# Head of the last stage of a decoder layer: second tile's scores directly behind the first's, its h turned on TensorE

## The reference, cut to what matters

```python
x = x + fake_quant(layernorm(x)) @ fake_quant(ctx)        # cross product, K = 1024
h = layernorm(x)
scores = (h @ Wq_w.T) @ keys.T                            # router: 16 wide, then 64 experts
gate = softmax over the 16 best scores, 0 elsewhere
z = h @ A_w.T                                             # 512 = 64 experts x 8
x = x + (z * gate) @ B_w.T * 2
```

## Time and profile before

| what | value |
|---|---|
| runs of before, us | 1106.42, 1109.94, 1109.15 (median 1109.15) |
| profiled execution, us | 1110.08, its span 1108.3 |
| TensorE busy | 1064.9 us, 96% of the span |
| VectorE busy | 905.2 us, 82% |
| ScalarE busy | 530.3 us, 48% |
| mean granted TensorE clock | 0.989 |

### The profile page before, as it was taken

One profiled execution on the slowest core, in us unless ns is written; L12 is line 12 of the kernel. 1 busy time (PEld: TensorE's weight loads), 2 busy tenths in 40 slices (PEclk: granted clock), 3 DMA queues, 4 the chain that ended last, 5 costly groups with the idle time before them and its releaser, 6 DMA issues.

```text
span 1108.3 us, 19648 instructions
## 1 busy us (share of the span) xinstructions
PE 1064.9 (96%) x6229; PEld 568.7 (51%) x6236; DVE 905.2 (82%) x1861; ACT 530.3 (48%) x1081; POOL 411.6 (37%) x423
## 2 busy tenths in 40 slices
PE   4999998999999999999999999999999998969998
PEld 3876544555555555555555555555555554434443
DVE  6789578988787978787888888787978798888973
ACT  4646366555454445454544455454545453233420
POOL 2049755534353434343442434353434243000000
PEclk8999999999999999999999999999999999989999
DMA  8016145654544445454545554554445378224442
GB/s 315 1 58 257 77 88 136 164 117 110 139 123 114 106 123 136 110 132 116 139 100 124 132 117 112 132 123 114 106 126 136 83 187 230 101 43 82 102 99 86
DMA packets 229601, 135.74 MB, mean 122 GB/s; under 512 B 200112, under 2 KB 202288, under 8 KB 228656
## 3 DMA queue, kind: packets, MB, share of 16 engines
q1 hardware_dynamic: 229552, 135.11, 48.1%
HBM read 68.23 MB, written 17.83 MB: 78 GB/s over the span
## 4 chain that ended last, share of the span: by engine, by line
PE 85%; DVE 8%; ACT 3%; issue 2%; DMA 1%; POOL 1%; SPq 0%; DVEq 0%; ACTq 0%; POOLq 0%
PE ps L1672 81%; PE ps L1924 2%; ACT prob L1034 1%; DVE wo_sb L1188 1%; DVE h_b L1188 1%; DVE prob L1397 1%; PE ps L1995 1%; DMA wq_sb<-wo_in 1%; DVE prob_t L1188 1%; DMA o_t<-in_wdown 1%; PE ps L1686 0%; ACT prob L890 0%; DVE stats L1196 0%; ACT wo_sb L807 0%; DVE wq_sb L1188 0%
## 5 line engine op out<-in xcount | busy, mean ns | idle before, releaser
L771 POOL TENSOR_SCALAR prob<-prob,row_inv 128x128 f32<-128x128 f32 (+3 forms) x256 | 203.5, 815 | 438.0 <-DVE row_inv L1368 438.0
L1672 PE MATMUL ps<-wo_sb,o_t 128*128 128x512 f16 x1536 | 353.0, 380 | 3.6 <-DVE x_sb L1379 3.6
L1672 PE MATMUL ps<-h_b,wq_sb 128*128 128x512 f16 x1524 | 344.9, 381 | 0.0
L1034 ACT ACTIVATE prob<-prob,neg_max 128x128 f32<-128x128 f32 (+3 forms) x256 | 140.6, 550 | 220.8 <-DVE neg_max L1403 220.8
L1672 PEld LDWEIGHTS ps<-h_b,wq_sb 128*128 128x128 f16 x1524 | 148.4, 98 | 178.2 <-issue 4.4
L1672 PEld LDWEIGHTS ps<-wo_sb,o_t 128*128 128x128 f16 x1536 | 147.6, 98 | 173.1 <-DVE x_sb L1379 6.3
L1379 DVE SCALAR_TENSOR_TENSOR x_sb<-ps,x_sb 128x512 f32<-128x512 f32 x256 | 174.2, 686 | 54.8 <-PE ps L1672 53.9
L1672 PE MATMUL ps<-prob_t,v_sb 128*128 128x128 f16 (+2 forms) x960 | 116.6, 274 | 6.5 <-DMA prob_t<-prob_s 6.5
L1672 PE MATMUL ps<-k_t,q_t 128*128 128x512 f16 (+3 forms) x768 | 114.8, 299 | 0.6 <-DVE neg_max L1403 0.5
L1397 DVE CUSTOM_DVE_ANT_0 prob<-ps,mask 128x512 f32<-128x512 f32 (+3 forms) x256 | 110.3, 484 | 2.3 <-issue 1.6
L1672 PEld LDWEIGHTS ps<-prob_t,v_sb 128*128 128x128 f16 x960 | 83.5, 98 | 36.8 <-DMA prob_t<-prob_s 7.3
(11 more groups left out here) (146 smaller groups left out, 1138.4 us busy)
## 6 DMA issues: line engine op xcount, KB each, us to landing
wq_in<-in_wq SPq DMA_DIRECT2D x64, 256.0 KB, 3.5
wo_in<-in_wo SPq DMA_DIRECT2D x32, 512.0 KB, 3.9
side_in<-in_ctx SPq DMA_DIRECT2D x16, 512.0 KB, 4.3
kv_parts<-wo_sb SPq DMA_DIRECT2D x7, 1024.0 KB, 5.0
x_sb<-in_x SPq DMA_DIRECT2D x8, 512.0 KB, 9.2
ctx_quantised<-side_out SPq DMA_DIRECT2D x16, 256.0 KB, 2.9
h_b<-ctx_quantised SPq DMA_DIRECT2D x2, 2048.0 KB, 10.8
out<-x_sb SPq DMA_DIRECT2D x8, 512.0 KB, 2.9
```

What stands on the lines that cost most here:

```text
L771: ins = nc.gpsimd.tensor_scalar(at, at, row_inv[:, u % 2, q:q + 1], S_P, ALU.mult, ALU.mult)
L1034: ins = nc.scalar.activation(at, at, ACT.Exp, bias=neg_max[:, n % 2, q:q + 1], scale=SOFTMAX, accum_out=row_sum[:, n % 2, q:q + 1])
L1672: ins = nc.tensor.matmul(out_, lhs(i), rhs(j), start=start and n == 0, stop=stop and n == 3 * len(pairs) - 1)
```

## The change

Only the last stage changes. On TensorE the h of tile 1 is now also turned there (`turn_h3(1)`, placed inside the z matmuls of `scores(0)`), `scores(1)` follows `scores(0)` directly, `x_product(2)` comes after it, and `scores(2)` moves behind `out_product(1)`. In every `scores` the keys now stand behind 6 matmuls of z, not 12. Thirteen matmuls whose result nobody reads (`fill`) stand around `turn_h3(0)`. The lists of ScalarE, VectorE and SyncE are written out by hand for tiles 0 to 3 to go with it; from i = 4 on the loop is as before. `gate_z` is the old body of the loop made a function. The diff, with that body left out on both sides:

```diff
--- before.py
+++ after.py
@@ -93,7 +93,12 @@
 
 def h3_dmas(t):
 
-    return 32 * ((t + t % 2) // 2)
+    return 32 * (t // 2)
+
+
+def h3_splits(t):
+
+    return 2 * t + 2 if t < 2 else t + 3
 
 
 def x_dmas(t):
@@ -108,6 +113,7 @@
 
 R_COL, S_COL = 0, P
 STEPS_AHEAD = 2
+TURN_FILL, ROUTER_FILL = 6, 7
 
 
 UNITS = GROUP * BATCH
@@ -629,12 +635,10 @@
                 sp.dma_start_transpose(blocks(x_qt[:, t % 2, :]), x_q[:, t % 2, :]).then_inc(x_landed[t % 2], 16)
 
             def turn_h3(t):
-                sp.wait_ge(h3_hi, t + 2)
-                sp.wait_ge(x_done, 2)
-                if t >= 2:
-                    sp.wait_ge(z_done, t - 1)
+                sp.wait_ge(h3_hi, h3_splits(t))
+                sp.wait_ge(z_done, t - 1)
                 sp.dma_start_transpose(blocks(h3_t[:, t % 2, 0, :]), h3_s[:, t % 2, 0, :]).then_inc(h3_landed[t % 2], 16)
-                sp.wait_ge(h3_lo, t + 2)
+                sp.wait_ge(h3_lo, h3_splits(t))
                 sp.dma_start_transpose(blocks(h3_t[:, t % 2, 1, :]), h3_s[:, t % 2, 1, :]).then_inc(h3_landed[t % 2], 16)
 
             def turn_gated(t):
@@ -645,18 +649,29 @@
                 sp.wait_ge(zt_lo, t + 1)
                 sp.dma_start_transpose(blocks(z_t[:, t % 2, 1, :]), z_s[:, t % 2, 1, :]).then_inc(z_landed[t % 2], 16)
 
+            def store(t):
+                sp.wait_ge(out_done, 2 * t + 2)
+                sp.dma_start(out[t], x_sb[:, t, :]).then_inc(stored, 16)
+
             turn_rounded(2)
-            for i in range(1, TT + STEPS_AHEAD):
+            turn_gated(0)
+            turn_rounded(3)
+            turn_gated(1)
+            turn_h3(2)
+            turn_rounded(4)
+            store(0)
+            turn_h3(3)
+            store(1)
+            turn_gated(2)
+            turn_rounded(5)
+            for i in range(4, TT + STEPS_AHEAD):
                 if i < TT:
                     turn_h3(i)
                 if i - 1 < TT - 1:
                     turn_gated(i - 1)
                 if i + STEPS_AHEAD < TT:
                     turn_rounded(i + STEPS_AHEAD)
-                if i >= 2:
-                    t = i - 2
-                    sp.wait_ge(out_done, 2 * t + 2)
-                    sp.dma_start(out[t], x_sb[:, t, :]).then_inc(stored, 16)
+                store(i - 2)
             sp.wait_ge(stored, 16 * TT)
 
         @block.gpsimd
@@ -1121,23 +1136,23 @@
 
             def h3_apply(t):
                 act.wait_ge(rstd3_done, t + 1)
-                if t == 2:
-                    act.wait_ge(h3_turned, 2)
-                if t >= 3:
-
-                    act.wait_ge(h3_hi, t)
-                    act.wait_ge(h3_lo, t)
+                if t in (2, 3):
+                    act.wait_ge(h3_turned, 2 * (t - 1))
+                if t >= 4:
+
+                    act.wait_ge(h3_hi, h3_splits(t - 2))
+                    act.wait_ge(h3_lo, h3_splits(t - 2))
                 nc.scalar.activation(h3[t % 2], x_sb[:, t, :], ACT.Identity, bias=h3_bias[:, t:t + 1],
                                      scale=rstd1[:, 2, 2 * TT + t:2 * TT + t + 1]).then_inc(h3_done, 1)
 
             def h3_high(t):
-                if t == 0:
+                if t < 2:
                     for j in range(2):
-                        act.wait_ge(h3_turned, j + 1)
-                        split_hi(h3_t[:, 0, 0, j * HALF:(j + 1) * HALF], ps[:, H_BANK[j], :], h3_hi, S_H)
+                        act.wait_ge(h3_turned, 2 * t + j + 1)
+                        split_hi(h3_t[:, t, 0, j * HALF:(j + 1) * HALF], ps[:, H_BANK[j], :], h3_hi, S_H)
                     return
                 act.wait_ge(h3_done, t + 1)
-                if t >= 3:
+                if t >= 4:
 
                     act.wait_ge(h3_landed[t % 2], h3_dmas(t - 2))
                 split_hi(h3_s[:, t % 2, 0, :], h3[t % 2], h3_hi, S_H)
@@ -1152,26 +1167,46 @@
                     act.wait_ge(z_landed[t % 2], z_dmas(t - 2))
                 split_hi(z_s[:, t % 2, 0, :], gated, zt_hi, 1.0)
 
-            h3_apply(0)
-            h3_high(0)
-            scale_rows(STEPS_AHEAD)
-            for i in range(1, TT + 1):
-                if i > 1:
-                    copy_small(i - 1)
-                if i < TT:
-                    h3_apply(i)
-                if i == 1:
-                    copy_small(0)
-                    sum_rows(STEPS_AHEAD)
-                t = i - 1
+            def weigh(t):
                 act.wait_ge(best_done, t + 1)
                 nc.scalar.activation(weight[:, t % 2, :], score[:, t % 2, :], ACT.Exp, bias=neg_best[:, t % 2:t % 2 + 1])\
                     .then_inc(weighted, 1)
+
+            h3_apply(0)
+            h3_high(0)
+            copy_small(0)
+            h3_apply(1)
+            h3_high(1)
+            scale_rows(2)
+            weigh(0)
+            sum_rows(2)
+            z_high(0)
+            scale_rows(3)
+            copy_small(1)
+            weigh(1)
+            z_high(1)
+            sum_rows(3)
+            h3_apply(2)
+            h3_high(2)
+            scale_rows(4)
+            sum_rows(4)
+            h3_apply(3)
+            h3_high(3)
+            scale_rows(5)
+            copy_small(2)
+            weigh(2)
+            z_high(2)
+            sum_rows(5)
+            for i in range(4, TT + 1):
+                copy_small(i - 1)
+                if i < TT:
+                    h3_apply(i)
+                weigh(i - 1)
                 if i < TT:
                     h3_high(i)
                 if i + STEPS_AHEAD < TT:
                     scale_rows(i + STEPS_AHEAD)
-                z_high(t)
+                z_high(i - 1)
                 if i + STEPS_AHEAD < TT:
                     sum_rows(i + STEPS_AHEAD)
 
@@ -1585,13 +1620,13 @@
                                                ALU.mult, ALU.mult).then_inc(rstd3_done, 1)
 
             def h3_split(t):
-                if t == 0:
+                if t < 2:
                     for j in range(2):
                         at = slice(j * HALF, (j + 1) * HALF)
-                        dve.wait_ge(h3_hi, j + 1)
-                        split_lo(h3_t[:, 0, 1, at], ps[:, H_BANK[j], :], h3_t[:, 0, 0, at], h3_lo, S_H)
+                        dve.wait_ge(h3_hi, 2 * t + j + 1)
+                        split_lo(h3_t[:, t, 1, at], ps[:, H_BANK[j], :], h3_t[:, t, 0, at], h3_lo, S_H)
                     return
-                dve.wait_ge(h3_hi, t + 2)
+                dve.wait_ge(h3_hi, h3_splits(t))
                 split_lo(h3_s[:, t % 2, 1, :], h3[t % 2], h3_s[:, t % 2, 0, :], h3_lo, S_H)
 
             def z_split(t):
@@ -1600,6 +1635,31 @@
                     split_lo(z_t[:, t % 2, 1, :], ps[:, ZT_BANK, :], z_t[:, t % 2, 0, :], zt_lo, 1.0)
                 else:
                     split_lo(z_s[:, t % 2, 1, :], gated, z_s[:, t % 2, 0, :], zt_lo, 1.0)
+
+            def gate_z(t):
...
             fold(0)
             x_half(0, 0)
@@ -1609,56 +1669,65 @@
             h3_split(0)
             turn3 = x_end(1)
             turn2 = quantise_start(2)
+            bias3(1, turn3)
             quantise_apply(2, turn2)
-            bias3(1, turn3)
+            h3_split(1)
             quantise_end(2)
-            for i in range(1, TT + STEPS_AHEAD):
-                if 1 < i < TT:
+            gate_z(0)
+            fold(2)
+            z_split(0)
+            turn2 = quantise_start(3)
+            quantise_apply(3, turn2)
+            gate_z(1)
+            quantise_end(3)
+            z_split(1)
+
+            x_half(2, 0)
+            turn3 = x_end(2)
+            turn2 = quantise_start(4)
+            bias3(2, turn3)
+            quantise_apply(4, turn2)
+            out_add(0, 0)
+            h3_split(2)
+            fold(3)
+            out_add(0, 1)
+            quantise_end(4)
+
+            x_half(3, 0)
+            turn3 = x_end(3)
+            turn2 = quantise_start(5)
+            bias3(3, turn3)
+            quantise_apply(5, turn2)
+            out_add(1, 0)
+            h3_split(3)
+            fold(4)
+            out_add(1, 1)
+            gate_z(2)
+            z_split(2)
+            quantise_end(5)
+
+            for i in range(4, TT + STEPS_AHEAD):
+                if i < TT:
                     x_half(i, 0)
                     turn3 = x_end(i)
                 if i + STEPS_AHEAD < TT:
                     turn2 = quantise_start(i + STEPS_AHEAD)
-                if 1 < i < TT:
+                if i < TT:
                     bias3(i, turn3)
                 if i + STEPS_AHEAD < TT:
                     quantise_apply(i + STEPS_AHEAD, turn2)
-                if 0 <= i - 1 < TT:
-                    t = i - 1
...
+                if i <= TT:
+                    gate_z(i - 1)
                 if i < TT:
                     h3_split(i)
                 if i + 1 < TT:
                     fold(i + 1)
-                if 0 <= i - 2 < TT:
-                    out_add(i - 2, 0)
+                out_add(i - 2, 0)
                 if i <= TT:
                     z_split(i - 1)
```

(97 more changed lines are left out.)

## The result

The changed kernel takes 1118.32 us (median of 4 runs, 1116.02 to 1119.11), the kernel before in the same comparison 1109.55. The ratio is 1.0083, with a 95% interval of 1.0064 to 1.0103: slower, by 8.8 us, where 8.9 was forecast (1118.0). The profiled execution, the slowest of the four, took 1119.11 us with a span of 1117.3; the forecast's sum gives 1119.0 and 1117.2 (1108.3 + 8.9). One slow execution of a later run, e1_copy1, took 2907.6 us and is left out of its ratio.

The account below looks back on a forecast made before the run. TensorE bounds the last stage, with time to win or lose only in its head. Two waits (8.45, 4.85 us) and 2.5 us of slow clock twice make 18.3, netting +8.9 us: 1118.0 us, range 1114 to 1121.5.

Parts of the forecast that it names:

- Place of the loss: Keys of tile 1: TensorE waits for ScalarE's copy_small(1), behind scale_rows(3), which waits for VectorE's ln2_done of tile 3.
- First wait: TensorE idle at the keys of tile 1 from 987.15 until ScalarE's copy ends at 995.6: 8.45 us.
- Second wait: TensorE idle at the keys of tile 2 for ScalarE's copy, behind h3_apply(3), h3_high(3) and scale_rows(5): 4.85 us.
- Z: The time when scores of tile 1 end on TensorE, worked out as 1002.35.
- Clock: TensorE's clock at half behind each of the two waits: 1.7 to 3.4 us lost each time, 2.5 taken.
- x_product(4): Cross product whose start shifts the end: forecast at 1033.8, before at 1024.90, so 8.9 us later.
- Hidden at no cost: Work claimed covered: fill within TensorE's waits, turning DMAs and store(0) in time, GpSimd's order kept, last gap staying 0.46 us.
- The copies do not hold TensorE: Rival: copies come right after their routers, so the kernel gets faster, 1103 us; chance 0.06.
- Only the first wait arises: Rival: VectorE's chain takes 20 us, not 25, so second wait and its slow clock go; 1110.7 us, chance 0.08.
- the clock does not fall: Rival: TensorE's clock stays up in the two waits, 5 us less: 1113 us; chance 0.04.
- The fill does not keep the clock up: Rival: clock at half behind tile 0's transposes, scores(0) loses 1.7 us, at most 3.4; 1119 to 1122 us, chance 0.08.

Follow-up runs that it names:

- e1: Changed kernel with copy_small(1) moved from behind to directly ahead of scale_rows(3) in ScalarE's list; 1112.08 us.
- e6: Changed kernel with VectorE's quantise_start(3) moved ahead of h3_split(1) and quantise_apply(3) directly behind it; 1113.52 us.
- e4: Changed kernel plus 36 and 20 matmuls whose result nobody reads in the waits at the keys of tiles 1 and 2; 1113.43 us.
- e3: Changed kernel with copy_small(1) moved ahead of scale_rows(3) and copy_small(2) ahead of h3_apply(3); 1109.36 us.
- e8: Changed kernel with both counts of fill set to 0; 1118.26 us.
- e2: Changed kernel with copy_small(2) moved from behind scale_rows(5) to between sum_rows(4) and h3_apply(3); 1114.82 us.
- e9: Kernel before with its own TensorE list and no fill, but VectorE's, ScalarE's and SyncE's lists rewritten for tiles 0 to 3; 1104.35 us.
- e5: Changed kernel with only VectorE's and ScalarE's lists for tiles 0 to 3 reordered, TensorE's and SyncE's kept; 1102.46 us.
- e7: Kernel before plus the change's thirteen fill matmuls and nothing else; 1109.72 us.

## Why the prediction was right

- **Place of the loss.** "TensorE needs `r_copied` of tile 1", behind `scale_rows(3)`: shown by the trace and, by cutting it at both ends, by e1 and e6.
- **First wait.** 8.45 us worked out, 8.10 measured. The stage began 0.78 us later in this execution (974.69 against 973.91), so the keys at 996.31 stand at 995.5 on the old scale, where 995.6 was worked out. TensorE's own wait for h of tile 1 was 0.46 and not 0.8.
- **Second wait.** 4.85 worked out, 5.00 measured. The chain of VectorE and ScalarE from Z, 24.65 us, came out at 24.6 (Z at 1002.96, the copy ends at 1027.52).
- **Clock.** 2.5 us twice. From the keys to the next cross product 6.65 us passed the first time and 6.39 the second (996.31 to 1002.96, 1027.57 to 1033.96), against 4.25 at full clock: 2.4 and 2.1. e4 confirms both from outside, with 4.26 and 4.25 us. The size of 2.5 was a choice between 1.7 and 3.4, and behind waits of 3.6 to 8.1 us in the other runs it came out from 1.6 (second wait of e1) to 2.8 (first of e6), so agreement to half a microsecond is partly chance. One reading behind it is slightly off: by the earlier trace rows the second slow stretch with work in it lasts 5.6 us and not 5.4, which changes nothing in the sum.
- **x_product(4).** Worked out 1033.8, measured 1033.96, or 1033.2 with the later start taken off. The forecast was some 0.6 us too high in the head: the first wait and both clock losses came out smaller and the second wait a little longer, 17.6 us in all where 18.3 was worked out. That the span still agrees to 0.1 us is luck: the stage happened to begin 0.78 us later in this execution. Behind `x_product(4)` nothing changed, 83.3 us against 83.4.
- **Hidden at no cost.** Fill, DMAs, SyncE's order, GpSimd's powers, keys behind six z: no wait of TensorE on any of them appeared in the head; the last gap, 0.46 us, is 0.44.
- **Rivals.** "The copies do not hold TensorE" is excluded by e1. Its price was too hopeful: with both copies moved (e3) the time is 1109.4 and not 1103. Up to `x_product(4)` the price nearly holds, 1019.4 on the old scale where `scores(2)` was to end at 1018.8. Behind it come 3.2 us of new waits at tile 3. The prediction's premise that whatever shifts `x_product(4)` shifts the end holds for the changed kernel, but not once TensorE runs that far ahead of VectorE. "Only the first wait arises" and "the clock does not fall" are excluded by the second wait of 5.00 us and by the granted clock behind both. "The fill does not keep the clock up" was priced at 1119 to 1122; the fill did keep it up (1.05 us for the router of tile 0). Without any fill e8 took 1118.26, so a fill that failed but cost nothing could not have been told from the forecast. The statement of the Trainium skill (TensorE: Matmul & The Clock Gate, Part 4) that transposes do not count as work for the clock agrees with e8, where the router behind them took 1.86 us. It is not tested there, since TensorE also stood idle for 1.44 us ahead of the transposes and 1.67 us behind them.

What stays open in part: e3's profiled head is 2.2 us shorter than before, its median is not shorter. The runs of one kernel lie up to 7 us apart (before: 1105.77 to 1112.70), and the mean granted clock differs between them: of these 23 executions the three at 0.998 took 1105.8 to 1106.6 us, the five at 0.989 1109.5 to 1112.7. The traces show where some of this arises, in the attention part and so outside the change. In e4's profiled execution the granted clock is 0.93 from 0 to 50 us, 0.93 from 150 to 200 and 0.97 from 900 to 950, in e2's 1.00, 0.97 and 1.00; with half clock as the lower level that makes some 17 us of slow clock against 3. It can cost up to half of that, 7 us more in e4 than in e2 as an estimate from these stretches, and e4's head began 4.2 us later (976.64 against 972.41). The head's length leaves that part out, while a difference of medians of 1 or 2 us can be the clock of the attention part. For e3's 2.2 us no run settles it.

## What to carry to other kernels

When a list of one engine is written out by hand, the cheap operation that another engine waits for (here a copy of 0.25 us) must not stand behind one that itself waits for a third engine: follow what stands ahead of it back to its last releaser. A better order on the busiest engine gives nothing while the lists that feed it stay late; the same rewriting of the feeding lists gave most of the gain with the old order too (e9, 5.5 us) and all of it with the new one (e5, 7.1). A wait costs more than its length where the clock falls in it, so a sum of waits alone is too small: here 13.1 us of waiting cost 17.6.

## What the runs showed of the hardware

Matmuls whose result nobody reads held the granted clock at 1.00 through waits of 8.1 and 5.0 us and took away the whole clock loss behind them in e4, 4.5 us by the timeline, although the work adds 12 us of its own to the busiest engine. The same means was worth nothing in e7, where a wait for another engine lay behind the slow stretch and took up what it cost; in e8 all but 0.55 us of it was taken up.

The length of a wait alone does not tell whether the clock falls. In e1, and the same in e3, it was at 0.50 behind a wait of 1.90 us, and 1.7 us were lost; behind the wait of 2.49 us of the kernel before and that of 2.54 us in e3 it stayed at 1.00. What else decides it, the runs do not separate.
